# Two float32r parts of Q and K, kept in both halves of the partitions, in place of three bfloat16 parts

## The reference

```python
Q = (content @ Wq).reshape(b, n, 16, 16)      # K and V alike, 16 heads of 16 features
scores = einsum('bqhd,bkhd->bhqk', Q, K) / sqrt(16)
alpha = softmax(scores, axis=-1)              # over all 2048 keys
alpha = where(tril, alpha, 0)                 # masked after the softmax
Y = einsum('bhqk,bkhd->bqhd', alpha, V)
x = layernorm(x + Y)
x = layernorm(x + moe(x))                     # top 2 of 8 experts, capacity 1280
```

## Time and profile before

| | |
|---|---|
| median of the runs | 1912.72 us |
| span of the profiled execution | 1938.8 us |
| another time of that execution | none is given; its span stands for it |
| projection stage | 0 to 101.7 us of the span |
| first score matmul of the attention | 119.7 us |
| end of the attention | about 1,097 us |
| PE busy, share of the span | 1658.6 us, 86% |
| ACT busy | 1268.4 us, 65% |
| DVE busy | 1151.0 us, 59% |
| mean granted TensorE clock | 0.932 of full speed |

### The profile page before, as it was taken

How to read it: one execution, slowest core, us unless ns; L and a number is a source line. 1 busy time by engine, 2 the same in 40 slices (tenths; PEclk the granted TensorE clock), 3 DMA queues, 4 the chain that set the end, 5 groups by cost and what they waited for, 6 DMA issues and landing times. The chain is left out here.

```text
span 1938.8 us, 31529 instructions
## 1 busy us (share of the span) xinstructions
PE 1658.6 (86%) x10758; PEld 1025.6 (53%) x10759; DVE 1151.0 (59%) x2219; ACT 1268.4 (65%) x1416; POOL 251.4 (13%) x251
## 2 busy tenths in 40 slices
PE   7848999999999999999999742099999999999990
PEld 6623433333333333334333442078988988889880
DVE  6855767768677676676877642045354444554533
ACT  7748999999999999999999710024233333332422
POOL 0000000000000000000000033612111221131111
PEclk9969999999999999999999855589999999999995
DMA  5577010100101101011010121333131412322016
GB/s 174 175 206 234 17 33 16 33 26 23 33 16 33 28 22 33 18 31 30 20 33 16 40 98 50 105 121 89 35 101 16 115 52 67 105 65 63 12 12 183
DMA packets 91081, 124.92 MB, mean 64 GB/s; under 512 B 10240, under 2 KB 76544, under 8 KB 91008
## 3 DMA queue, kind: packets, MB, share of 16 engines
q1 hardware_dynamic: 76416, 106.85, 17.4%
q0 software_dynamic: 14592, 17.06, 4.8%
HBM read 74.78 MB, written 51.18 MB: 65 GB/s over the span
## 5 line engine op out<-in xcount | busy, mean ns | idle before, releaser
L697 ACT ACTIVATE probs<-scores 128x1536 f32<-128x1536 f32 (+1 forms) x384 | 520.6, 1379 | 48.7 <-PE scores L627 43.5
L627 PE MATMUL scores<-aq,ak 98*128 98x512 bf16 (+3 forms) x1280 | 304.1, 352 | 61.5 <-DMA aq<-shift_dram 26.8
L740 DVE TENSOR_REDUCE sums<-expq 128x1 f32<-128x1408 f32 (+6 forms) x448 | 347.3, 827 | 13.8 <-ACT expq L703 13.8
L643 PE MATMUL o_ps<-probs,vh 128*32 128x512 f32 (+3 forms) x2560 | 340.0, 543 | 0.0
L1386 ACT ACTIVATE gate<-up_ps 128x512 f32<-128x512 f32 x128 | 76.5, 598 | 350.8 <-PE up_ps L1278 348.6
L627 PE MATMUL scores<-ak,aq 98*128 98x512 bf16 (+3 forms) x1184 | 264.5, 343 | 17.0 <-ACT probs L697 9.0
L703 ACT ACTIVATE expq<-scores 128x1536 f32<-128x1536 f32 x192 | 274.8, 1449 | 2.0
L627 PEld LDWEIGHTS scores<-aq,ak 98*128 98x128 bf16 x1280 | 96.8, 98 | 235.4 <-ACT probs L697 72.8
L627 PEld LDWEIGHTS scores<-ak,aq 98*128 98x128 bf16 x1184 | 91.2, 98 | 238.5 <-ACT expq L703 94.7
L727 DVE TENSOR_TENSOR hidden<-probs,after 128x384 f32<-128x384 f32 x128 | 70.9, 554 | 243.9 <-ACT probs L697 243.9
L1278 PE MATMUL up_ps<-xeT_hi,wup_hi 128*128 128x512 f32 x512 | 205.7, 402 | 11.4 <-issue 9.9
(11 more groups left out here) (209 smaller groups left out, 2378.8 us busy)
## 6 DMA issues: line engine op xcount, KB each, us to landing
raw<-w_T SPq DMA_DIRECT2D x16, 1024.0 KB, 10.0
split_dram<-parts SPq DMA_DIRECT2D x48, 256.0 KB, 2.9
aq<-split_dram SPq DMA_DIRECT2D x192, 64.0 KB
xe_dram<-blank SPq DMA_DIRECT2D x1, 10560.0 KB, 56.1
raw<-wg_T SPq DMA_DIRECT2D x8, 1024.0 KB, 8.7
xin<-xe_dram SPq DMA_DIRECT2D x8, 792.0 KB, 5.5
ak<-split_dram SPq DMA_DIRECT2D x32, 192.0 KB
xin<-xe_dram SPq DMA_DIRECT2D x8, 528.0 KB, 3.8
```

The costliest lines, as they stand in the source:

```text
L627: last = nc.tensor.matmul(dst[:, at:at + w], still, moving[0:KS, lo:lo + w], start=True, stop=True, skip_group_check=True)
L643: last = nc.tensor.matmul(dst[32 * r:32 * r + 32, BLK - w:BLK], vh[j % 2][:, k, :], probs[:, m % P_RING, at:at + w], start=first, stop=Tru ...
L697: last = nc.scalar.activation(probs[:, m % P_RING, 0:w], src[:, 0:w], ACT.Exp, scale=HD ** -0.5)
L740: last = nc.vector.tensor_reduce(sums[:, j % 2, col:col + 1], expq[:, n % X_RING, at:at + w], AX.X, ALU.add)
```

## The change

Q and K are kept in two float32r parts (high, and the rest), which together hold the value. The third part, `rest`, the middle copy on ACT and the second subtraction on DVE are gone, and the shift is stored once as float32r. A head's operands have 49 rows: high-high, low-high and high-low (3 x 16), and one row for the shift. They are loaded twice, to partitions 0 to 48 and to 64 to 112. Each score matmul takes both operands from one of the halves: the first for the even PSUM banks of its tile, the second for the odd one. The constant row of `ak` comes by DMA from a row that POOL fills.

```diff
-            parts = sb(st, "parts", [P, 3, U, N], BF16)
-            rest = sb(st, "rest", [P, 2, BLK])
+            parts = sb(st, "parts", [P, 2, U, N], FP32R)
...
-            shift = sb(st, "shift", [H, 2, T], BF16)
+            shift = sb(st, "shift", [H, T], FP32R)
...
-                        for s in range(3):
+                        for s in range(2):
                             sp.dma_start(split_dram[i, s, b * D:(b + 1) * D, cols].rearrange("(c p) t -> p c t", p=P),
...
-                            pe.wait_ge(proj_read, i * (2 * U) + (j * U + u + 1))
+                            pe.wait_ge(proj_split, i * (2 * U) + (j * U + u + 1))
...
-                        if u >= 1:
-                            act.wait_ge(proj_read, at + U)
-                            nc.scalar.activation(parts[:, 1, u - 1, cols], rest[:, (u - 1) % 2, :], ACT.Copy).then_inc(mid_ready, 1)
...
-                            nc.vector.tensor_tensor(rest[:, u % 2, :], proj[:, u, :], hi[u], ALU.subtract).then_inc(proj_read, 1)
-                        if u >= 1:
-                            dve.wait_ge(mid_ready, at)
-                            nc.vector.tensor_tensor(lo[u - 1], rest[:, (u - 1) % 2, :], mid[u - 1], ALU.subtract).then_inc(proj_split, 1)
+                        nc.vector.tensor_tensor(parts[:, 1, u, cols], proj[:, u, :], parts[:, 0, u, cols].bitcast(FP32), ALU.subtract).then_inc(proj_split, 1)
...
-                    nc.vector.tensor_copy(shift[:, 0, b * N:(b + 1) * N], bound[:]).then_inc(dve1, 1)
-                    dve.wait_ge(dve1, step + 5)
-                    nc.vector.tensor_tensor(shift[:, 1, b * N:(b + 1) * N], bound[:], shift[:, 0, b * N:(b + 1) * N],
-                                            ALU.subtract).then_inc(shift_ready, 1)
+                    nc.vector.tensor_copy(shift[:, b * N:(b + 1) * N], bound[:]).then_inc(shift_ready, 1)
...
-        aq = [sb(att, f"aq{j}", [P, N], BF16) for j in range(2)]
-        ak = [sb(att, f"ak{j}", [P, N], BF16) for j in range(2)]
-        KR = 6 * HD
-        KS = KR + 2
+        aq = [sb(att, f"aq{j}", [P, N], FP32R) for j in range(2)]
+        ak = [sb(att, f"ak{j}", [P, N], FP32R) for j in range(2)]
+        KR = 3 * HD
+        KS = KR + 1
+        HALVES = (0, P // 2)
+        AQ = (0, 1, 0)
+        AK = (0, 0, 1)
...
+            for at in range(3):
+                rows = slice(row + at * HD, row + (at + 1) * HD)
+                sp.dma_start(aq[j][rows, :].bitcast(FP32), split_dram[0, AQ[at], bass.ds(n * HD, HD), :]).then_inc(done, 16)
+                sp.dma_start(ak[j][rows, :].bitcast(FP32), split_dram[1, AK[at], bass.ds(n * HD, HD), :]).then_inc(done, 16)
...
+                    for row in HALVES:
+                        load_operands(sp, j, n, row, a_loaded[j])
+                        sp.dma_start(aq[j][row + KR:row + KS, :].bitcast(FP32), shift_dram[bass.ds(n, 1), :]).then_inc(a_loaded[j], 16)
 
                 for j in range(2):
                     load_head(j, j)
+                sp.wait_ge(minus_ready, 1)
+                for j in range(2):
+                    for row in HALVES:
+                        sp.dma_start(ak[j][row + KR:row + KS, :].bitcast(FP32), minus[:].bitcast(FP32)).then_inc(minus_stored, 16)
...
+                pool.memset(minus[:].bitcast(FP32), -1.0 / HD ** -0.5).then_inc(minus_ready, 1)
...
-                pe.wait_ge(minus_ready, 2)
+                pe.wait_ge(minus_stored, 64)
...
-                    for at, still, moving, lo, w in pieces:
-                        last = nc.tensor.matmul(dst[:, at:at + w], still, moving[0:KS, lo:lo + w], start=True, stop=True, skip_group_check=True)
+                    for at, still, col, moving, lo, w in pieces:
+                        row = HALVES[at // BLK % 2]
+                        last = nc.tensor.matmul(dst[:, at:at + w], still[row:row + KS, col:col + P], moving[row:row + KS, lo:lo + w], start=True, stop=True, skip_group_check=True)
...
-                for j in range(2):
-                    nc.vector.memset(ak[j][KR:KS, :], -1.0 / HD ** -0.5).then_inc(minus_ready, 1)
```

More of the change, by code:

```diff
@@ L352, in one_block @@
                     if b > 0:
-                        act.wait_ge(parts_stored[2 * i + j], 16 * 6)
+                        act.wait_ge(parts_stored[2 * i + j], 16 * 4)
                     act.wait_ge(norm_ready, i * 2 + (b * (NB // B) + j + 1))
                     cols = bass.ds(i * (2 * BLK) + j * BLK, BLK)
-                    for u in range(U + 1):
+                    for u in range(U):
                         at = i * (2 * U) + (b * (U * NB // B) + j * U + u)
[L359 to L362, removed]
-                        if u >= 1:
-                            act.wait_ge(proj_read, at + U)
-                            nc.scalar.activation(parts[:, 1, u - 1, cols], rest[:, (u - 1) % 2, :], ACT.Copy).then_inc(mid_ready, 1)
+                        act.wait_ge(proj_ready, at + 1)
+                        nc.scalar.activation(sq[:, u, :], proj[:, u, :], ACT.Square).then_inc(sq_ready, 1)
+                        nc.scalar.activation(parts[:, 0, u, cols], proj[:, u, :], ACT.Copy).then_inc(hi_ready, 1)
                     for t in range(4):
@@ L445, in program, with load_operands @@
         attn = sb(att, "attn", [P, 2, NT, HD])
-        aq = [sb(att, f"aq{j}", [P, N], BF16) for j in range(2)]
-        ak = [sb(att, f"ak{j}", [P, N], BF16) for j in range(2)]
-        KR = 6 * HD
-        AQ = ((0, 3), (1, 2), (2, 1))
-        AK = ((0, 3), (3, 2), (5, 1))
-        KS = KR + 2
-        A_DMAS = 6 + 3
-        def load_operands(sp, j, n, done):
-            for s, (part, times) in enumerate(AQ):
-                for r in range(times):
-                    at = (0, 3, 5)[s] + r
-                    sp.dma_start(aq[j][at * HD:(at + 1) * HD, :], split_dram[0, part, bass.ds(n * HD, HD), :]).then_inc(done, 16)
-            for at, k in AK:
-                sp.dma_start(ak[j][at * HD:(at + k) * HD, :], split_dram[1, 0:k, bass.ds(n * HD, HD), :]).then_inc(done, 16)
+        aq = [sb(att, f"aq{j}", [P, N], FP32R) for j in range(2)]
[5 more added lines that the diff above has]
+        AK = (0, 0, 1)
+        A_DMAS = 6
+        def load_operands(sp, j, n, row, done):
+            for at in range(3):
+                rows = slice(row + at * HD, row + (at + 1) * HD)
+                sp.dma_start(aq[j][rows, :].bitcast(FP32), split_dram[0, AQ[at], bass.ds(n * HD, HD), :]).then_inc(done, 16)
+                sp.dma_start(ak[j][rows, :].bitcast(FP32), split_dram[1, AK[at], bass.ds(n * HD, HD), :]).then_inc(done, 16)
         g_loaded, g_link, g_scores, g_read = sem("g_loaded"), sem("g_link"), sem("g_scores"), sem("g_read")
@@ L545, in program @@
             pairs = NH // 2
+            LOADS = 2 * (A_DMAS + 1)
             @block.sync
@@ L618, in fill @@
                         for g, k, at, w in KT[m]:
-                            pieces.append((at, ak[j][0:KS, k * P:(k + 1) * P], aq[j], (g + 1) * BLK - w, w))
+                            pieces.append((at, ak[j], k * P, aq[j], (g + 1) * BLK - w, w))
                     else:
```

51 lines of the change are left out of this document (21 added, 30 removed).

## The result

The changed kernel takes 1953.33 us (median of 4 runs, 1949.20 to 1965.18), the kernel before beside it 1911.55 us: the ratio is 1.0219 [1.0181, 1.0256], 41.8 us slower where 19.3 us faster was forecast. The profiled execution took 1965.18 us, with a span of 1963.4 us, 12 us over the kernel's own median.

A forecast was written before the change was run, and what follows sets the result against it. ACT was taken as the bound (98.4% busy in steady attention), PE a close second. Terms -5.0 - 2.3 + 2.5 - 7.2 - 7.3 = -19.3 us off 1912.7 gave 1893 us; 8-in-10 range 1882 to 1916.

The forecast's parts named there:

- rival 3: Attention: PE, less busy, is granted half clock; a head near 48 us, over 500 us more; chance 0.04.
- The start: First load's issue to first score matmul: about 16 us instead of 13.5, +2.5 us, bounds +1 and +7.7.
- Head 2: ACT's stall before head 2 goes because its loads land in time: -7.2 us, bounds 0 and 7.2.
- The score matmuls: Attention: matmuls in separate row halves overlap, a fill of three takes two's time; saves PE 4.8 us a head.
- the price of float32r: Score matmuls: the type costs at most 0.01 us a matmul, 0.8 us a head of PE.
- The switch of shape: Turns between score fills: eight new shape changes a head at 0.10 us each, costing PE 0.8 us a head.
- The steady heads: ACT's 0.25 us wait at a head's first fills goes: -7.3 us over 29 heads, bounds 0 and 14.
- The projection: PE's stall between batches goes, -5.0 us; L437's wait at the end of batch 1 goes, -2.3 us.

The follow-up runs named there:

- e5: The kernel before with its bf16 score matmuls cut to rows 0 to 48 of 98: 2015.2 us profiled, 2045.8 us in a second run, against 1913.4.
- e6: The changed kernel with 64 rows used in each half, rows 49 to 63 set to zero: 1919.8 us, ratio 1.0043.
- e7: The changed kernel with the odd bank's score matmul made twice in each fill whose second bank is one 512-column piece: 1914.8 us, ratio 1.0008.
- e1: The changed kernel with operands loaded once and all score matmuls in one half, partitions 0 to 48: 2509.7 us, ratio 1.313.
- e3: The changed kernel with all matmuls of one fill in the same half, changing from fill to fill: 2101.3 us profiled and 2155.8 us.
- e11: The changed kernel with the constant rows' DMAs ahead of the loads and 64 rows per half, zeros made on two engines: 1909.7 us, ratio 0.9989.
- e2: The changed kernel with each score matmul over partitions 0 to 112, both halves at once, the exponential's scale halved: 1984.4 us, ratio 1.038.
- e12: e11 with head 2's loads queued ahead of filling xe_dram and head 3's ahead of the expert weights: 1891.56 us, ratio 0.9898.
- e9: The changed kernel with a head's two parts adjacent in DRAM, so one DMA fills 32 rows, stores cut finer: 1969.6 us, ratio 1.029.

## Why the prediction was wrong

**The step that failed is the clock.** The sum took every duration of the attention at full clock, and rival 3 was set at 0.04 because "the clock stood at 1.00 in the steady heads with PE idle for a few tenths at a time, and no gap grows to more than about 1 us". The gaps are indeed no longer (0.57 us at most ahead of the fall at 488 us): the clock fell all the same, at a price of 54.8 to 58.7 us. The argument asked how long TensorE pauses. What the runs show is how much of the array works: 49 rows in place of 98 lowers the clock in bf16 as well (e5, 0.90), 15 rows of zeros or a matmul repeated beside the others bring it back (e6, 1.00; e7, 0.98) with the same pauses, and with one half alone it stays near 0.6 at 98.5% busy (e1). Why one half alone (0.60) does so much worse than the halves by turns (e3, 0.89) stays open. The price in rival 3 was off too: it had half clock for good, over 500 us; in the changed kernel it comes and goes, in 13 heads of 28, by 1.5 to 6.4 us each. The Trainium skill, "TensorE: Matmul & The Clock Gate", Part 1, puts the clock down to how busy TensorE has been and warns of idle gaps. By that rule nothing would happen here, or in e1; the granted clock of 0.61 at 236.51 us busy of 240 speaks against reading "busy" as the busy time of the profile.

**The start was mis-sized**: +2.5 forecast with an upper bound of 7.7, +17.5 measured. The issue was right (12.1 us for 28 loads, 12.4 to 13 forecast). The transfer was not costed. From 131 GB/s at a share of 0.52 I took it that half of the engines had room. An estimate shows how that row misleads: six DMAs of 64 KB issued in 2.66 us offer 148 GB/s, so little could wait; with 128 KB at each issue of 0.44 us nearly 300 GB/s are offered. But 24 loads of 128 KB are 3.15 MB, at 123 GB/s 25.6 us, and after the change the rate is the same, 107 to 131, with the share doubled. The prediction did ask PE to wait for the constant rows behind head 1, which doubled the bytes it waits for. The rule for the number of engines that the prediction uses for `ak` stands in "DMA: Bandwidth & Descriptors" of the Trainium skill under another section than it names, "Why a DMA increments its semaphore by 16 and not by 1".

**Head 2** came out as forecast, -7.25 us, but not for the reason given. Loads were to be issued 64 us after the first load and to land at 77, for a need at 79. In e11 they are issued at 169.72, 68 us after the first load at 102.03, and land at 193, 91 us after it. It is the late start that hid this: with the start near the forecast one, ACT stands for 13.5 us. Start and head 2 together could not have brought the forecast -4.7.

**The score matmuls**: the mechanism, that row halves overlap, was right, and so was its size: it takes 0.96 - 0.73 = 0.23 us off a fill of three, where one start of 0.218 was forecast. What was mis-sized is the price of float32r, taken from the projection's rows as 0.01 us a matmul, 0.02 in a fill of three. In the same rows, without overlap, such a fill takes 0.96 us (e1, e2) against 0.82 in bf16, 0.14 more. So it comes out at 0.73 us, forecast 0.6 to 0.65. The switch of shape, forecast 0.8 us a head, measures 0.96 (e5; the changed kernel's turns have the same distances, 0.66 us from a fill that is 0.09 shorter, and 0.58 to the next fill). PE's work in a head fell from 28.6 us to 221.39 / 240 x 29.77 = 27.5 (e12), by 1.1, not 3.3. This cost nothing, since ACT is the bound.

**The steady heads**: -0.25 us each forecast, -0.41 measured (30.18 to 29.77), inside the bound of 0.48. ACT's wait for `probs` is gone; in e12 a smaller one stands in its place:

```profile
ACT expq L699 <- PE scores L623: 4.5, 28, 0.2
```

ACT's idle time in a head went from 0.48 to 6.79 / 800 x 29.77 = 0.25 us. The rest is ACT's own work, 236.18 / 240 x 30.18 = 29.70 us a head before and 793.21 / 800 x 29.77 = 29.52 in e12; its exponentials are the same, and why they take less is open.

**The projection**: -7.3 forecast, -8.56 measured, by the steps given: 5.4 between the batches (forecast 5.0) and 3.1 behind them (2.3).

With the clock and the start set right, and the queue's order changed besides, which was no part of the change, the terms sum to about what was forecast: e12 is 20.9 us under the kernel before, 1891.6 us for a forecast of 1893. That is partly chance: e12's start is where it was before (119.59 and 119.69 us), not 5 us sooner, and its heads are 5 us better than forecast.

## What to carry to other kernels

A matmul that uses fewer of the array's rows can cost clock even while TensorE is busy 93% of the time; look at the granted clock by windows of a few microseconds in the lightest part of the loop, and if it falls, try filling the unused rows with zeros, which here took no time in the matmuls. Cost a transfer by its bytes over the rate seen for the same number of partitions, not by the share of busy DMA engines. When a start is made earlier, look at what the next loads stand behind in their queue: what was hidden by a late start shows then.

## What the runs showed of the hardware that I had not expected

- The granted clock depends on the rows in use: 98 rows 1.00, 49 rows in bf16 0.90, 113 rows of float32r 1.00, 64 rows in two overlapping halves 1.00, 49 rows in two overlapping halves 0.93, in two halves by turns 0.89, in one half 0.60 (means from 200 to 1000 us). The rows added in e6 held zeros, and did it all the same. Only these points were measured; what lies between them is open, and so is what makes one half so much worse than two by turns.
- Loads into 16 partitions together move 107 to 131 GB/s whether half or all of the DMA engines are shown as busy; with two thirds of the bytes in loads into 32 (e9), 113 to 197; while `x_sb` goes into 128, 334 to 351.
- When TensorE goes from score matmuls of 49 rows to a transpose of 128 and back, it loses 0.09 and 0.15 us (e5 against the kernel before).
- A float32r weight load of 49 to 113 rows takes 0.19 us, a bf16 one of 98 rows 0.10, and three float32r score matmuls in the same rows take 0.96 us where bf16 ones take 0.82.
- A DMA issue can hold its queue for 20 to 32 us (`xe_dram` 22.07, `wg_T` 31.59) when it is issued behind transfers still on their way, and took 0.66 and 0.38 us when issued later; in e12 a load of 128 KB behind `xe_dram` took 11.36 us. That a full queue is the reason was not tried by itself.
